# Third attention of a decoder on one core: shifted scores of batches 4 to 7 as float32r products of packed 12-bit key and query parts

## What is computed

```python
Q = _split(query @ W_q.T)
K = _split(key @ W_k.T)
V = _split(value @ W_v.T)
scores = jnp.einsum('bhqd,bhkd->bhqk', Q, K) / jnp.sqrt(jnp.float32(D_K))
scores = jnp.where(mask, -jnp.inf, scores)
attn_w = jax.nn.softmax(scores, axis=-1)
out = jnp.einsum('bhqk,bhkd->bhqd', attn_w, V)
```

## Time and profile before

| | |
|---|---|
| median of 3 runs | 403.53 us (403.22 to 405.26) |
| span of the profiled execution | 401.2 us; its own time is not printed |
| TensorE busy | 364.8 us (91%) |
| VectorE busy | 275.4 us (69%) |
| ScalarE busy | 231.2 us (58%) |
| GpSimd busy | 142.3 us (35%) |
| DMA | 13.86 MB, mean 35 GB/s |
| third attention | about 257 to 306 us |

### The profile page before, as it was taken

How to read it: one execution, slowest core, us unless ns; L and a number is a source line. 1 busy time by engine, 2 the same in 40 slices (tenths; PEclk the granted TensorE clock), 3 DMA queues, 4 the chain that set the end, 5 groups by cost and what they waited for, 6 DMA issues and landing times.

```text
span 401.2 us, 10126 instructions
## 1 busy us (share of the span) xinstructions
PE 364.8 (91%) x4066; PEld 249.6 (62%) x4066; DVE 275.4 (69%) x713; ACT 231.2 (58%) x439; POOL 142.3 (35%) x130
## 2 busy tenths in 40 slices
PE   4989997788999999999999999699997999999991
PEld 2556675566766747556777777456774566666671
DVE  6867978656658786789898886765766444444446
ACT  2855568676776367899999972145564512221210
POOL 6929962571340420048799781200012000000002
PEclk9999999999999999999999999999999999999997
DMA  6420000000000000303223210450000000000001
GB/s 175 92 56 2 4 2 2 2 3 2 5 0 2 0 2 2 110 30 99 84 80 118 80 39 2 149 168 3 3 5 0 2 0 2 0 1 2 0 2 52
DMA packets 16882, 13.86 MB, mean 35 GB/s; under 512 B 6548, under 2 KB 14133, under 8 KB 16837
## 3 DMA queue, kind: packets, MB, share of 16 engines
q1 hardware_dynamic: 15538, 12.51, 10.5%
q10 hardware_dynamic: 1299, 0.71, 0.6%
HBM read 12.64 MB, written 0.57 MB: 33 GB/s over the span
## 4 chain that ended last, share of the span: by engine, by line
PE 76%; ACT 10%; DVE 8%; issue 3%; POOL 1%; POOLq 0%; DVEq 0%
PE PS L1990 10%; PE PS L2078 7%; PE PS L2082 7%; PE PS L1566 7%; PE PS L2109 7%; PE PS L1505 6%; PE PS L1977 5%; PE PS L1586 4%; PE PS L1545 4%; ACT att L659 3%; PE PS L1511 3%; PE PS L1635 2%; PE PS L1789 2%; PE PS L1569 2%; DVE untransposed L1304 2%
## 5 line engine op out<-in xcount | busy, mean ns | idle before, releaser
L659 ACT ACTIVATE att<-PS 77x512 f32<-77x512 f32 (+1 forms) x96 | 51.7, 592 | 41.0 <-PE PS L1569 41.0
L1040 DVE TENSOR_REDUCE mxp<-PS 128x4 f32<-128x308 f32 (+1 forms) x96 | 48.2, 536 | 20.2 <-PE PS L1545 20.1
L906 ACT ACTIVATE kM<-PS 128x512 f32<-128x512 f32 x32 | 19.1, 597 | 55.4 <-PE PS L2078 55.4
L506 POOL TENSOR_TENSOR rstd<-ve,neg_half 128x4 f32<-128x4 f32 x6 | 6.2, 1025 | 103.9 <-DVE ve L936 103.9
L1355 DVE TENSOR_TENSOR_SCAN big<-big,PS 128x768 f32<-128x768 f32 x22 | 38.3, 1748 | 5.2 <-PE PS L1977 4.8
L512 POOL TENSOR_TENSOR rstd<-ve,neg_half 128x1 f32<-128x1 f32 x24 | 14.2, 593 | 76.6 <-DVE ve L977 76.6
L1444 DVE TENSOR_TENSOR big<-kM,PS 128x512 f32<-128x512 f32 x32 | 21.9, 688 | 27.3 <-PE PS L2082 26.0
L2078 PE MATMUL PS<-xT,V 128*128 128x512 f32 x64 | 33.0, 596 | 1.1 <-DVE xT L1432 0.8
L2082 PE MATMUL PS<-xT,V 128*128 128x512 f32 x64 | 32.7, 592 | 0.0
L2109 PEld LDWEIGHTS PS<-big 128*128 128x128 f32 x256 | 29.7, 192 | 3.3 <-issue 3.3
L2109 PE MATMUL PS<-big 128*128 128x128 f32 x256 | 29.7, 275 | 0.0
(11 more groups left out here) (366 smaller groups left out, 860.4 us busy)
## 6 DMA issues: line engine op xcount, KB each, us to landing
kM<-Cdram SPq DMA_DIRECT2D x6, 384.0 KB, 3.5
XH<-Cdram SPq DMA_DIRECT2D x5, 384.0 KB, 3.4
xT<-Cdram SPq DMA_DIRECT2D x5, 384.0 KB, 3.4
V<-in_L_ffn_Wg SPq DMA_DIRECT2D x1, 1024.0 KB, 5.5
V<-in_L_ffn_Wu SPq DMA_DIRECT2D x1, 1024.0 KB, 8.1
out_x<-X SPq DMA_DIRECT2D x2, 256.0 KB, 2.3
ctxN<-in_ctx ACTq DMA_DIRECT2D x1, 308.0 KB
X<-in_x SPq DMA_DIRECT2D x1, 256.0 KB, 3.5
```

What stands on the lines that cost most here:

```text
L659: A_(PT[0:nk, i % 2, g], bank4(at.bank("exp", i, g), nk), ACT.Exp, scale=at.scale)\
L1040: V_.tensor_reduce(mxp[:, b % 3, g, 0:J], PS[:, at.bank("max", b, g), 0:J * nk].rearrange("p (j k) -> p j k", j=J), axis=AX.X, op=ALU.max) ...
```

## The change

For batches 4 to 7, `shifted` multiplies packed operands of type float32r: `K4` and `Q4`, [128, 4, ...], in which each head fills a whole row group with 4 parts x 8 channels. Keys and queries are split into a high part (rounded to 12 bits by a copy to float32r) and the exact rest. Keys are stacked as (high, low, high, low), queries as (high, high, low, low), so that the 32 rows sum all four cross products. There are as many products as before; row group g and step j now stand for head 4j + g, so for these batches the maxima, values and normalised outputs are placed in the transposed order of (g, j).

The packing goes through DRAM: GpSimd splits, SP stores four parts (four DMAs) into `k_packed` or `q_packed`, and GpSimd loads them back in one DMA with a cast to float32r. For the keys this stands between GpSimd's preparations and the scan; GpSimd also makes the four masked copies of k5.1, and VectorE only copies it out of PSUM. For the queries it stands after q5.1, ahead of `attention_pool`, and SP's four stores stand ahead of the experts' loads. New waits: GpSimd for the stores, ScalarE's scale(0) and VectorE's PaT copy for the stores of the keys, TensorE for the loads in each packed batch.

```diff
+F32R = mybir.dt.float32r
...
+class Packed:
+    def keys(self, g, j, b):
+        i = b - self.first
+        return self.K[32 * g:32 * g + 32, j, i * self.nk:(i + 1) * self.nk]
+    def queries(self, g, j, b):
+        i = b - self.first
+        return self.Q[32 * g:32 * g + 32, j, i * T:(i + 1) * T]
...
+    K4 = sb("K4", [128, G, HB * NC], F32R)
+    Q4 = sb("Q4", [128, G, HB * T], F32R)
+    k_packed = nc.dram_tensor("k_packed", [G * 128, HB * NC], F32, kind="Internal").ap()
+    q_packed = nc.dram_tensor("q_packed", [G * 128, HB * T], F32, kind="Internal").ap()
+    key_high, key_low = (t[:].rearrange("p b t -> p (b t)")[:, 0:HB * NC] for t in (XB, qT))
+    query_high, query_low = (t[:, HB:B, :].rearrange("p b t -> p (b t)") for t in (sq, XH))
+    key_raw = mix3[:, 0:HB * NC]
+    KEYS_SPLIT, KEYS_MASKED, QUERIES_SPLIT = 2, 3, 5
... SP, after the first loads
+        def pack(dst, parts):
+            rows = dst.rearrange("(h c d) n -> c h d n", c=4, d=HD)
+            for c, part in enumerate(parts):
+                sp.dma_start(rows[c], part, allow_slow_non_contiguous=True).then_inc(event("packed_stored"), 16)
+        sp.wait_ge(event("split"), KEYS_SPLIT)
+        pack(k_packed, [key_high, key_low, key_high, key_low])
         sp.wait_ge(event("proj_copied"), 2)
...
+        sp.wait_ge(event("split"), QUERIES_SPLIT)
+        sp.wait_ge(event("packed_stored"), 4 * 16)
+        pack(q_packed, [query_high, query_high, query_low, query_low])
         sp.wait_ge(dring.full, dring.index["dl.1"] + 1)
... GpSimd, after its preparations
+        def split(x, high, low, done):
+            P_.tensor_copy(high.bitcast(F32R), x).then_inc(event("split"), 1)
+            pool.wait_ge(event("split"), done - 1)
+            P_.tensor_tensor(out=low.bitcast(F32R), in0=x, in1=high, op=ALU.subtract).then_inc(event("split"), 1)
+        def unpack(dst, src, n):
+            pool.wait_ge(event("packed_stored"), 4 * 16 * n)
+            P_.dma_start(dst[:], src.rearrange("(g p) n -> p g n", g=G).bitcast(F32R),
+                         allow_slow_non_contiguous=True).then_inc(event("packed_loaded"), 16)
+        dring.wait_copied(pool, "k5.1")
+        split(key_raw, key_high, key_low, KEYS_SPLIT)
+        for j in range(J):
+            ins = P_.tensor_scalar(out=kM5[:, j, HB:B, :], in0=key_raw.rearrange("p (b n) -> p b n", b=HB),
+                                   scalar1=headmask[:, j:j + 1], scalar2=None, op0=ALU.mult)
+        ins.then_inc(event("split"), 1)
+        pool.wait_ge(event("split"), KEYS_MASKED)
+        unpack(K4, k_packed, 1)
... and after the scan's products
         rstds()
+        aring.wait_copied(pool, "q5.1")
+        split(qT[:, HB:B, :].rearrange("p b t -> p (b t)"), query_high, query_low, QUERIES_SPLIT)
+        unpack(Q4, q_packed, 2)
         attention_pool(at5)
... ScalarE, scale(0); the same wait on VectorE ahead of the copy to PaT
+                act.wait_ge(event("packed_stored"), 4 * 16)
... VectorE
+            heads = oN[:, n % 2, :].rearrange("p (j g d) -> p g j d" if at.packs(n) else "p (g j d) -> p g j d", g=G, j=J)
+            V_.tensor_tensor(heads, out_heads(at, n)[:, :, 0:HD].rearrange("p (g j) d -> p g j d", g=G),
...
+                V_.tensor_reduce(mxp[:, b % 3, 0:G, g] if at.packs(b) else mxp[:, b % 3, g, 0:J],
...
-        i = take("k5.1")
-        for j in range(J):
-            ins = V_.tensor_scalar(kM5[:, j, HB:B, :], PS[:, i, 0:HB * NC].rearrange("p (b n) -> p b n", b=HB),
-                                   headmask[:, j:j + 1], None, ALU.mult)
-        ins.then_inc(dring.copied, 1)
+        V_.tensor_copy(key_raw, PS[:, take("k5.1"), 0:HB * NC]).then_inc(dring.copied, 1)
... TensorE, shifted(b)
+                if at.packs(b):
+                    pe.wait_ge(at.packed.loaded, 16 * 2)
                 for j in range(J):
                     for g in range(G):
+                        if at.packs(b):
+                            keys, queries = at.packed.keys(g, j, b), at.packed.queries(g, j, b)
+                        else:
+                            keys, queries = at.kM[rows(g), j, b, :], qT[rows(g), b, :]
+                        M_(PS[0:nk, at.bank("exp", b, g), j * T:(j + 1) * T], keys, queries, start=not at.masked, stop=False)
... weigh(b): at.V[0:nk, b, J * j + g if at.packs(b) else J * g + j, :]; ahead of the third attention:
+        pe.wait_ge(event("split"), KEYS_MASKED)
```

More of the change, by code:

```diff
@@ L109, with __init__ @@
 PLACE = {slot: n for n, slot in enumerate(SLOTS)}
+class Packed:
+    def __init__(self, first, nk, K, Q, loaded):
+        self.first, self.nk, self.K, self.Q, self.loaded = first, nk, K, Q, loaded
+    def keys(self, g, j, b):
[4 more added lines that the diff above has]
+        return self.Q[32 * g:32 * g + 32, j, i * T:(i + 1) * T]
 class Attention:
-    def __init__(self, sem, name, nk, scale, kM, V, Wo, XB, Xout, masked=False, late=None):
+    def __init__(self, sem, name, nk, scale, kM, V, Wo, XB, Xout, masked=False, late=None, packed=None):
         self.nk, self.scale, self.kM, self.V = nk, scale, kM, V
@@ L118, in __init__ @@
         self.late = late
+        self.packed = packed
         self.scores_ready = sem(f"{name}_scores_ready")
@@ L141, in bank, with packs @@
         return RING_BANKS[PLACE[what, i, g] % len(RING_BANKS)]
+    def packs(self, b):
+        return self.packed is not None and b >= self.packed.first
     def out_bank(self, b):
@@ L291, in _build @@
     at2 = Attention(sem, "at2", NC, math.sqrt(HD), kM2, V2, Wp2[:], XB, X[0], late=event("q_late"))
-    at5 = Attention(sem, "at5", NC, 1 / math.sqrt(HD), kM5, V5, W5T[:, 3, :], X[0], X[1], masked=True)
+    K4 = sb("K4", [128, G, HB * NC], F32R)
[6 more added lines that the diff above has]
+    KEYS_SPLIT, KEYS_MASKED, QUERIES_SPLIT = 2, 3, 5
+    at5 = Attention(sem, "at5", NC, 1 / math.sqrt(HD), kM5, V5, W5T[:, 3, :], X[0], X[1], masked=True,
+                    packed=Packed(HB, NC, K4, Q4, event("packed_loaded")))
     def upper(t):
@@ L1016, in normalise @@
                 dve.wait_ge(at.flipped_ready, n + 2)
-            V_.tensor_tensor(oN[:, n % 2, :].rearrange("p (h d) -> p h d", h=H), out_heads(at, n)[:, :, 0:HD],
-                             rs[:, n % 2, :].rearrange("p (h o) -> p h o", o=1).to_broadcast([128, H, HD]),
+            heads = oN[:, n % 2, :].rearrange("p (j g d) -> p g j d" if at.packs(n) else "p (g j d) -> p g j d", g=G, j=J)
+            V_.tensor_tensor(heads, out_heads(at, n)[:, :, 0:HD].rearrange("p (g j) d -> p g j d", g=G),
+                             rs[:, n % 2, :].rearrange("p (g j o) -> p g j o", g=G, o=1).to_broadcast([128, G, J, HD]),
                              ALU.mult).then_inc(at.normed, 1)
@@ L1039, in maximum @@
                     dve.wait_ge(at.flipped_ready, b - 2)
-                V_.tensor_reduce(mxp[:, b % 3, g, 0:J],
+                V_.tensor_reduce(mxp[:, b % 3, 0:G, g] if at.packs(b) else mxp[:, b % 3, g, 0:J],
                                  PS[:, at.bank("max", b, g), 0:J * nk].rearrange("p (j k) -> p j k", j=J),
@@ L1363, in _ @@
                 dve.wait_ge(event("turned"), 3 - m)
+                dve.wait_ge(event("packed_stored"), 4 * 16)
                 V_.tensor_copy(half(PaT, m), bank4(3)).then_inc(event("turned_copied"), 1)
@@ L1563, in shifted @@
                                .to_broadcast([32, J, 32]), start=False, stop=False)
+                if at.packs(b):
+                    pe.wait_ge(at.packed.loaded, 16 * 2)
                 for j in range(J):
                     for g in range(G):
-                        M_(PS[0:nk, at.bank("exp", b, g), j * T:(j + 1) * T], at.kM[rows(g), j, b, :], qT[rows(g), b, :],
-                           start=not at.masked, stop=False)
+                        if at.packs(b):
[3 more added lines that the diff above has]
+                        M_(PS[0:nk, at.bank("exp", b, g), j * T:(j + 1) * T], keys, queries, start=not at.masked, stop=False)
                     for g in range(G):
@@ L1585, in weigh @@
                     for j in range(J):
-                        ins = M_(PS[32 * j:32 * j + 32, at.out_bank(b), 128 * g:128 * g + 128], at.V[0:nk, b, J * g + j, :],
+                        ins = M_(PS[32 * j:32 * j + 32, at.out_bank(b), 128 * g:128 * g + 128], at.V[0:nk, b, J * j + g if at.packs(b) else J * g + j, :],
                                  PT[0:nk, b % 2, g, j, :], start=True, stop=True)
```

## The result

The changed kernel took 413.43 us in the median of four runs (411.72 to 415.25), the kernel before 403.41 on the same chip: a ratio of 1.022, interval 1.0175 to 1.0263. The profiled execution took 413.23 us with a span of 411.2, against 401.2. The forecast of 402.3 and the range up to 406.0 both missed.

A forecast was written before the change was run, and what follows sets the result against it. TensorE was taken to bound the kernel, busy for 91% of the span, with batch 4 an unbroken run on it. The terms -2.7 + 0.3 + 0.9 + 0.3 = -1.2 us gave span 400.0, time 402.3, range 401.0 to 406.0.

The forecast's parts named there:

- The products: Third attention, batches 4 to 7: float32r scores cost what bf16 costs, 0.68 us less a batch, -2.7 us.
- Given back at the maxima: Transposes of the maxima (L1604), batches 5 and 6: TensorE waits for VectorE's remainders, about 0.3 us returned.
- The keys: Key stage: GpSimd's added work holds up one VectorE compare, +0.9 us (0.1 to 2.7).
- Rival 2: Key stage: every GpSimd op holds VectorE for its whole length, +0.6 us net, 404.1 us; chance 0.17.
- The queries: Ahead of batch 4: Q4 lands at 281.2 to 283.8, asked for at about 282.9; stall 0.3 us (0 to 1.0).
- Rival 4: At shifted(4) on TensorE: Q4 lands 3.9 us late through slow GpSimd issue, +2.4 us net, 405.9 us; chance 0.13.
- released by a DMA: Sign that the forecast is wrong (rival 4): a gap of several us ahead of shifted(4), ended by a DMA.
- another clock: Whole kernel: a different hardware clock was named as something not foreseen, with no size given.

The follow-up runs named there:

- as_changed: The changed kernel once more, unaltered: 411.96 us (4 runs), ratio 1.018 to the kernel before.
- kept_busy: The changed kernel with 26 bf16 products of zeros ahead of TensorE's wait for Q4: 407.85 us, ratio 1.009 to the kernel before.
- masks_on_vector: experts_first with the four masked key products moved from GpSimd back to VectorE: 402.01 us, ratio 0.9935; in a second series 403.83 us, ratio 0.9986.
- experts_after_q4: The changed kernel with SyncE's three expert loads held back until Q4 has landed: 407.26 us (10 runs), ratio 1.002 to the kernel before.
- experts_first: The changed kernel with the expert loads put back ahead of the query stores: 402.35 us (10 runs), ratio 0.9955 to the kernel before.
- load_on_sync: The changed kernel with the queries' load issued by SyncE, ahead of the experts' loads: 407.65 us (10 runs), ratio 1.005 to the kernel before.

## Why the prediction was wrong

The sum, on the executions without another fall of the clock (as_changed 409.2, before 401.2), step by step:

- **The products**, put at -2.7. With the clock at full speed (kept_busy), the mask lines of batches 5, 6 and 7 start at 293.86, 298.42 and 301.84, and the experts' first product at 310.20: 4.56, 3.42 and 8.36 us, where it was 5.15, 4.05 and 8.99 before. That is 0.59 to 0.63 a batch, 2.5 over four. The step has a pitch of 0.13 us instead of 0.29. Mechanism and size were right; batch 5's 4.56 lies in the forecast's 4.5 to 4.6. The Trainium skill, page "FP8 and Floating Point Precision", section "TensorE Precision Notes", gives four passes for true float32; the trace's ratio of 0.23 to 0.07 us, 3.3, is near that, and for float32r the page has no number.
- **Given back at the maxima**, put at +0.3: nothing. The slack of 0.58 us in the earlier trace rows took in the 0.6 to within a few hundredths: in kept_busy the second remainder of that step ends at 296.17 and the load of the transpose starts at 296.22.
- **The keys**, put at +0.9: 0.7 (176.1 against 175.35 at the first L684, and back to 175.4 in masks_on_vector); 0.1 of it stood already at 75 us, ahead of the keys. The place was right and the form was not. I took one op held up for 0.9 us. In the trace three of VectorE's nine compares are longer, L1342 by 0.22 us, one L1344 by 0.26 and another by about 0.2, and the other six are not (ns min/median/max, VectorE's compares and GpSimd's masks):

```profile
L1344 DVE SCALAR_TENSOR_TENSOR V<-big,scol,after x8: 339/340/603, 148.8 to 151.1; 128x128 bf16<-128x128 f32 x8
```

```profile
L671 POOL TENSOR_SCALAR kM<-mix,headmask x4: 1050/1152/1479, 146.2 to 149.8; 128x308 f32<-128x308 f32 x4
```

  Rival 2 is out. The Trainium skill, page "SBUF — State Buffer", section "Who interferes with whom", gives a whole-instruction lock for a VectorE op with two SBUF inputs against a GpSimd op that reads SBUF. The trace does not agree: L1342 started at 147.41, in the midst of a mask op (147.28 to 148.33), and ended at 148.86, so it cannot have stood still until that op was done. Beside it the mask op took 1.05 us, as long as the one before, which ran while VectorE had almost nothing to do.
- **The queries**, put at +0.3: this is the step that failed. The forecast had them stored at 275.7 and Q4 there at 281.2 to 283.8. In as_changed the load was issued at 277.9 and landed at 289.6, and TensorE waited for 5.9 us. The stores began at 270.96, as forecast, but took 0.6 us each to issue and not 0.4, and were all landed only 6.6 us later and not 4.7: that and the hand-over make the 2.2 us up to the issue. The larger part is the load: I took 5.5 to 8.1 us from the earlier trace rows, where three transfers stand on one queue. I did write that the 3.1 MB move over the same time, but priced it by a row of one queue. Here the queries came in on a second queue, while the first had most of 3 MB to move, and took 11.6. The list of queues of as_changed shows where (packets, MB, share of the 16 engines), from 277.9 to 282.4 us and from 284 to 288:

```profile
q1 hardware_dynamic: 1561, 1.59, 107.6%
...
q0 software_dynamic: 1, 0.00, 0.1%
```

```profile
q1 hardware_dynamic: 342, 0.68, 58.9%
q0 software_dynamic: 355, 0.72, 54.5%
```

  For 4.5 us after its issue the queries' queue (q0) moved one packet, while the experts' moved 1.59 MB. In experts_after_q4, with nothing beside it, the first packets came 1.5 us after the issue (281.5 against 279.99). From then to the landing it took 7.1 us here and 4.5 there, since each queue now had half. So of the 5.6 us beyond 6.0, about 3.0 are the late start and 2.6 the shared bandwidth. The Trainium skill, page "DMA: Bandwidth & Descriptors", section "Queues, rings and completion order", says that each DMA engine goes round the queues that have work, packet by packet; the trace agrees once both move. Why the first packets came so late beside the other queue stays open. Rival 4 named the place and the sign, and needed 1.5 us of lateness to decide. Its reason, that an issue by GpSimd is slow in itself, fell with experts_after_q4 (6.0 us, in the range that I had taken), and its 3.9 us were 5.9.
- **The clock**, not in the sum: +3.5. I priced a wait by its length alone. The prediction even wrote that another clock "would be nothing that I foresaw".

So -2.5 + 0.7 + 5.9 + 3.5 = 7.6 of the measured 8.0; the other 0.4 I don't assign. The predicted gap "released by a DMA" ahead of shifted(4) is the sign that came.

All but 0.7 us of what the change cost was thus no part of what it computes. It came from moving three loads, which had landed with no other bulk transfer beside them (255 to 265 us), behind a wait on the same queue. One thing in the prediction's own words should have given warning: SyncE's loads "now start at about 272.7", and Q4 was due 10 us later.

## What to carry to other kernels

Before a DMA or a wait is put into a queue, list what stands behind it there and when that will move instead: a transfer on the critical path should never share its window with a bulk load that could have gone earlier. Price two loads in flight on two queues at half the bandwidth each, and count on a later start of the second one (here 4.5 us from issue to the first packets, 1.5 alone). Price a wait of several us on a busy TensorE at more than its length, since the clock that it loses is paid for afterwards. And if such a version loses, try the same work in another order before you give up the idea: here the order alone was worth 8 to 10 us.

## What was not expected of the hardware

- After a wait of 5.9 us TensorE ran at half clock for 9 us more (the clock was down from 288.5 to 298.7 us in as_changed), though it was busy without a gap from 290 on. The fall cost 3.5 us, over half of the wait itself. It also fell after a wait of 1.2 us in experts_first (289.0 to 292.3) and after the stop of 2.25 us in experts_after_q4 (299.8 to 303.0), and did not after a wait of 1.0 us in load_on_sync.
- TensorE stopped for 2.1 and 2.25 us inside straight runs of products (L1648, L1663), where the program has no wait, in just the two kernels where the experts' loads pass under its work of batches 4 and 5, and started again as that traffic ended. In the third attention of the others no such stop is over 0.3 us, also in kept_busy, where zeros were multiplied beside 350 GB/s. The list of queues of load_on_sync has one packet of some 16 KB of the instruction queue in 288 to 290 us, with the DMA engines over 100% taken; that instructions came late behind data is my reading, and no run tested it.
- GpSimd's mask product of 128x308 took 1.05 us even with VectorE almost idle, against 0.44 for its copy of the same size; beside VectorE's compares the four took up to 1.48. VectorE lost 0.66 us over 3.4. Both sides are slowed at times, and neither stands still for an instruction of the other.
- float32r on 32-row tiles: one record for each product, a pitch of 0.13 us for four products and their four bf16 partners, against 0.29 with float32. How many bits a part keeps in the copy to float32r, no run here measures.
